# Order of the splits and of the exchange of accumulators at the middle of a decoder's self-attention stage

## The reference

```
q = rope(x @ wq.T)                       # 32 heads of 128
k_full = concat(k_cache[block_idx], k)   # 8 key heads, 512 + 64 keys
v_full = concat(v_cache[block_idx], v)
out = softmax(q @ k_full.T / sqrt(128)) @ v_full
x = layernorm(x + out @ wo.T)
```

## Time and profile before

| | |
|---|---|
| time, median of 3 runs | 2948.93 us (2946.65 to 2952.25) |
| the profiled execution | 2950.85 us, its span 2949.0 us |
| TensorE matmuls | busy 2817.6 us, 96% |
| VectorE | busy 1835.9 us, 62% |
| ScalarE | busy 1505.4 us, 51% |
| GpSimd | busy 1487.9 us, 50% |
| chain that ended last | TensorE 57%, VectorE 25%, ScalarE 7%, issue 6% |
| self-attention stage | marks of period 0 at 89.59 us, of period 63 at 1682.00 us |

### The profile page before, as it was taken

The page is one execution under the profiler, slowest core; times in us unless marked ns, Lnnn a source line. Parts: engine busy times, 40 slices in busy tenths (PEclk is TensorE's granted clock), DMA queues, the critical chain, the costliest instruction groups (busy, mean ns, idle before and its releaser), DMA issues.

```text
span 2949.0 us, 68202 instructions
## 1 busy us (share of the span) xinstructions
PE 2817.6 (96%) x28800; PEld 2538.0 (86%) x28800; DVE 1835.9 (62%) x3289; ACT 1505.4 (51%) x3202; POOL 1487.9 (50%) x1261
## 2 busy tenths in 40 slices
PE   4899999999999999999999989999999999999997
PEld 3788888888888888888888888999999999999976
DVE  4566666676666666666666665655555566555566
ACT  4456556565555665555555634433344444343344
POOL 6577768777766666666666732112123312121124
PEclk8999999999999999999999999999999999999999
DMA  4233133223325212321222231111111111111101
GB/s 147 58 100 99 52 94 104 72 81 100 84 80 156 84 46 82 84 83 45 82 85 77 62 95 42 34 41 40 33 41 57 51 33 47 33 40 33 30 19 58
DMA packets 108874, 197.98 MB, mean 67 GB/s; under 512 B 25112, under 2 KB 35608, under 8 KB 108568
## 3 DMA queue, kind: packets, MB, share of 16 engines
q1 hardware_dynamic: 88856, 154.81, 18.5%
q10 hardware_dynamic: 17664, 34.61, 3.4%
q0 software_dynamic: 2048, 4.20, 0.6%
HBM read 176.78 MB, written 16.78 MB: 66 GB/s over the span
## 4 chain that ended last, share of the span: by engine, by line
PE 57%; DVE 25%; ACT 7%; issue 6%; POOL 2%; DMA 1%; ACTq 1%; SPq 1%; DVEq 0%; POOLq 0%
PE big L1693 25%; PE bank L1693 14%; PE bank L1785 12%; DVE nmx L1307 7%; DVE P L1313 5%; DVE xacc L1335 4%; PE big L1785 3%; DVE rall L1329 3%; DVE qTl L1302 2%; ACT qTh L846 2%; PE big L1765 2%; ACT P L891 2%; ACT oTh L906 1%; ACT pth L900 1%; ACTq L911 1%
## 5 line engine op out<-in xcount | busy, mean ns | idle before, releaser
L726 POOL TENSOR_TENSOR ptl<-P,pth 128x576 fp32r<-128x576 f32 x512 | 724.6, 1434 | 193.6 <-ACT pth L900 192.6
L891 ACT ACTIVATE P<-big,nmx 128x576 f32<-128x576 f32 x512 | 379.2, 741 | 321.6 <-DVE nmx L1307 319.0
L1313 DVE STREAM_TRANSPOSE P<-P 128x576 f32<-128x576 f32 x512 | 386.5, 764 | 69.0 <-ACT P L891 69.0
L1785 PE MATMUL bank<-pth,vh 32*128 32x256 f32 x2304 | 368.4, 288 | 55.9 <-issue 27.4
L1307 DVE TENSOR_REDUCE nmx<-big 128x1 f32<-128x576 f32 x512 | 377.0, 747 | 4.7 <-PE big L1765 3.4
L900 ACT ACTIVATE pth<-P 128x576 fp32r<-128x576 f32 x512 | 347.2, 681 | 48.4 <-DVE P L1313 48.2
L1785 PE MATMUL bank<-pth,vl 32*128 32x256 f32 x2304 | 363.4, 283 | 0.2
L1785 PE MATMUL bank<-ptl,vh 32*128 32x256 f32 x2304 | 362.3, 283 | 1.1 <-issue 1.1
L1785 PE MATMUL big<-pth,vh 32*128 32x256 f32 x2304 | 341.1, 289 | 0.6 <-issue 0.4
L1785 PE MATMUL big<-pth,vl 32*128 32x256 f32 x2304 | 334.5, 283 | 1.0 <-issue 1.0
L1785 PE MATMUL big<-ptl,vh 32*128 32x256 f32 x2304 | 333.9, 282 | 0.3 <-issue 0.3
(11 more groups left out here) (282 smaller groups left out, 9276.7 us busy)
## 6 DMA issues: line engine op xcount, KB each, us to landing
rall<-kept_r ACTq DMA_DIRECT2D x64, 512.0 KB, 3.7
raw<-in_wo SPq DMA_DIRECT2D x64, 256.0 KB, 3.0
raw<-in_wq SPq DMA_DIRECT2D x62, 256.0 KB, 2.8
raw<-in_xWq SPq DMA_DIRECT2D x33, 256.0 KB, 2.7
raw<-in_xWo SPq DMA_DIRECT2D x32, 256.0 KB, 2.7
rawb<-in_xWo SPq DMA_DIRECT2D x32, 256.0 KB, 2.7
rawb<-in_xWq SPq DMA_DIRECT2D x31, 256.0 KB, 2.8
vh<-kept_vh SPq DMA_DIRECT2D x28, 224.0 KB, 4.2
```

What stands on the lines that cost most here:

```text
L726: pool.tensor_tensor(third_columns(ptl, i), blocks_of(i), f(third_columns(pth, i)), ALU.subtract).then_inc(p_low(i), 1)
L891: act.activation(P[:, i % PSLOTS, :].rearrange("p (k n) -> p k n", k=2), ps_s[i % 2][:, :, 0:HALF], ACT.Exp, bias=nmx[:, i % 8:i % 8 + 1], ...
L1313: dve.transpose(P[:, i % PSLOTS, :], P[:, i % PSLOTS, :]).then_inc(p_turned(i), 1)
L1785: m = pe.matmul(ps_o[a][:, 0:256], v[r, s, :], p[r, lo:hi + 1:hi - lo, b, :, :], start=first, stop=final)
```

## The change

The blocks x8 and x9 are split early in period 29, no longer late. wq34 is split late in period 31, before wq35, no longer late in period 30. SyncE makes the exchange of a part one period later than before: that of part 0 at the end of its period 31, behind the late values and the keys, that of part 1 at the end of its period 32. The order of the loads follows the plan.

```
@@ split_plan
-        if 2 <= k + 4 < GROUPS:
-            late.append(("wq", k + 4))
+        if 2 <= k + 4 < GROUPS and k != 30:
+            late += [("wq", 34), ("wq", 35)] if k == 31 else [("wq", k + 4)]
...
-        early += {30: [("x", 10), ("x", 11)], 31: [("x", 14), ("x", 15)]}.get(k, [])
-        late += {29: [("x", 8), ("x", 9)], 30: [("x", 12), ("x", 13)], 60: [("xwk", 0), ("xwq", 0)],
+        early += {29: [("x", 8), ("x", 9)], 30: [("x", 10), ("x", 11)], 31: [("x", 14), ("x", 15)]}.get(k, [])
+        late += {30: [("x", 12), ("x", 13)], 60: [("xwk", 0), ("xwq", 0)],
@@ sync_program
-                if k in (30, 31):
-                    p = part(k)
-                    gate.wait_ge(acc_done, (k, 3))
+                if k in (31, 32):
+                    p = part(k - 1)
+                    gate.wait_ge(acc_done, (k - 1, 3))
```

## The result

The changed kernel took 2942.14 us (median of 8 runs, 2938.67 to 2943.93) against 2952.19 of the kernel before beside it (8 runs, 2946.65 to 2953.71). The ratio is 0.9969, 95% interval 0.9959 to 0.9979: faster by 0.31%. In a second comparison it was 0.9979 (0.9968 to 0.9991), with medians of 2937.89 (8 runs) and 2944.6 (14 runs). The profiled execution took 2939.41 us with a span of 2937.6.

A forecast was written before the change was run, and what follows sets the result against it. TensorE, busy 96% of the span, bounds the kernel; periods 29 to 31 hold 11.0 us above the quiet pace. 4.21 + 1.2 + 2.84 + 0.6 = 8.85 us gives 2940.1 us, range 2937.5 to 2942.5, with slow-side rivals 2936.5 to 2945.5.

The forecast's parts named there:

- Period 29, 4.21 predicted: Splitting x8 and x9 beside values(29) removes 2.72 us of delay and, with the idle time, 1.49 of clock fall.
- The clock's 1.49: Period 29: values(30) lasts 1.49 us more because TensorE's granted clock fell after idle time; claimed to go.
- Period 30, 1.2 predicted: Without wq34, x12's copy starts 0.52 us earlier and VectorE's low part shortens from 1.37 us; gain 1.2.
- the upper bound: Period 30: gain of 1.34 us if VectorE's low part of x12 takes only 0.55 us.
- a rival with 0.13: The fall of the clock moves to period 30, or runs mostly had none in period 29; 2941.6 us, chance 0.13.
- a sign of being wrong: A lower granted clock in period 30 of the changed profile would show the prediction wrong.
- Period 31, 2.84 and 0.6 predicted: Late values issued 5.4 us earlier end TensorE's wait, 2.84; half of the 1.25 us inside values(32), 0.6.
- the other rival: The sums wait behind the exchange, holding period 32's mark by 2.1 to 5.7 us; 2942 to 2946 us, chance 0.16.
- the named signs: Wrong if: sums' DMA releases normalise_out(32), ScalarE lacks raw data in 29 or 31, lower clock in 30, period 31 above 26 us.
- The second late split, 0 predicted: Period 31 with wq34 and wq35 both late: slack just swallows one more copy of 0.53; cost 0, bound 0.5 us.
- The exchange off the path: Exchange behind the late values and keys: load back in by 938.2, add_out(32, 0) needs it about 939; cost 0.
- the crowd: Transfers in flight together: late values landed in 5.3 to 6.4 us there, the sums' spreading took 8.0 us.

The follow-up runs named there:

- store first and wait later: Kernel before, part 0's accumulator store still ahead of the late values, wait and load back behind the keys, part 1's exchange one period later; periods 29 to 31: 80.52 us.
- the two kernels that store first: Part 0's exchange split, store ahead of the late values: on the kernel before (periods 29 to 31 80.52 us), and on changed with x12 low on GpSimd (ratio 0.9962).
- plan only: Changed kernel with the new plan of splits but the exchange where it was before; ratio to before 0.999, periods 29 to 31 82.00 and 81.21 us.
- the lows on GpSimd: Kernel before with the low parts of x8 and x12 on GpSimd instead of VectorE, still late; ratio to before 0.9977.
- exchange only: Kernel before with the exchange moved one period later and the plan of splits as before; ratio to before 0.9991.

## Why the prediction was right

The time moved by 0.31%, and in the second comparison by 0.21%; the forecast was 0.30%, inside both intervals. By its steps:

- **Period 29, 4.21 predicted, 4.21 measured.** The delay of 2.72 went and so did the fall of the clock. The early place costs nothing: period 29 took 24.70 to 24.82 us in all ten profiles with x8 and x9 early. The clock's 1.49 is the weaker part, since "store first and wait later" shows the old plan without a fall.
- **Period 30, 1.2 predicted, 1.18 measured, and 1.49 lost.** The low part was shortened as worked out from GpSimd's end, though alone it takes 0.69 us, and not the 0.55 of the upper bound: the 0.55 is only what is left of it when GpSimd has ended. The clock, which the sum held at full speed, fell behind the smaller gap that remains: TensorE was busy 4.21 of 5 us there, and granted 0.74 and 0.83 afterwards. The period got 0.31 longer. That was a rival with 0.13, and it took place beside the forecast, not in its stead. A lower clock in period 30 was also named as a sign of being wrong, and both profiles of the changed kernel show it.
- **Period 31, 2.84 and 0.6 predicted, 2.84 and 1.25 measured** in the first profile: the stall inside values(32) went whole. Taking half of it was a guess, and its reason, full DMA engines, is not borne out: the DMA share was 0.34 and then 0.07 within that stall (932.8 to 933.7), 1.04 and 1.07 within those of the two kernels that store first, and 1.05 over 930 to 934 in the second profile of "plan only", where values(32) has no stall. In the second profile 1.7 us came back as the wait for the sums, the other rival, near the lower end that it was given (2.1). With it came two more of the named signs, the sums' DMA as the releaser of `normalise_out(32)` and a period 31 above 26 us.
- **The second late split, 0 predicted.** In the changed kernel values(32) begins 17.92 us after the mark, with wq34 and wq35 both late. Right.
- **The exchange off the path.** Right for `add_out`, even with 1 MB more ahead of it; not always right for the sums. The prediction took the crowd as the danger and did not ask which of the spreading and the load back goes out first.

The forecast was near for a reason that is partly luck. The sum 8.85 holds 1.49 for a clock that moved to the next period, so the periods gave 8.00 and 6.34 us, and the rest of the 10 us between the medians lies where executions differ anyway.

What stays open: whether the fall in period 30 belongs to the kernel. It came in three of three profiles with the changed order of periods 29 and 30 and the moved exchange, and in none of two with the plan alone, whose gap is the same (0.79 and 0.80 us). Three and two are too few to call it a rule. Open as well is why values(32) is stopped in its middle in some kernels: 0.92 us in the one before, 0.56 and 1.00 in the two that store first, 0.71 with the lows on GpSimd, and not at all in those with the exchange moved whole. (That is the idle time in the row; values(32) is longer by 0.33 us more each time, so by the 1.25 of the prediction in the kernel before.) All four have a store of the accumulators issued ahead of the late values, but so has "plan only", and neither of its two profiles has the stop. So the store is not enough to cause it, and that the change removed it is not shown.

## What to carry to other kernels

A queue that waits for its own transfer stops everything behind it: what made the values late was 5.4 us of waiting, with the load back put ahead of them adding to it, and not the 1 MB stored. Look for the consumer with the least slack behind each such wait, and after a move look for it again, since here it became the sums. Before a split or a copy is moved in time, ask which engine's place between two steps of the main chain it takes: another engine's name in one line brought 5.9 us, and in the end the last 3 us as well.

When a change is worth 0.3%, cut the profile at marks of its own. Periods 0 to 28, which no edit touched, took 756.96 and 764.03 us in two profiles of one kernel on two chips, while the three periods that were touched took 74.12 and 74.14.

## What the runs showed of the hardware

- The clock does not follow the gap's length alone. Behind the gaps at the end of period 30 with 1.6 us idle (0.79 and 0.80) the granted clock of the next 4 us fell to 0.61 to 0.74 in three profiles and stayed at 1.00 in two; behind the seven with 2.4 us (1.59 and 0.80) in periods 29 and 30 it fell in three. In "exchange only" a fall in period 29 cost 2.7 us in all where the others cost some 1.5.
- From the issue of the sums' store of 16 KB to that of their spreading, which waits for it, ScalarE needs 4.5 us in the quiet period 32 of the changed kernel (942.01 to 946.51), but 5.0 to 7.1 beside a 1 MB store in the kernels with the exchange moved, and 8.9 beside two (913.53 to 922.40).
- The spreading itself, 512 KB, lands in 3.5 to 5.0 us when it is issued ahead of a 1 MB load on SyncE's queue and in 6.0 to 6.6 when it is issued 0.1 to 0.3 us behind it (seven profiles).
- The same program has periods of 24.70 or of 25.45 us in one and the same place, constant within an execution over many of them (periods 3 to 19 with k % 4 == 3). In these runs the longer ones came on one chip of three.
